# Attention with stationary probabilities, a column of ones beside the values, and two turns before the output projection

## What is computed

```
q, k, v = split(layernorm(x) @ qkv_w.T)          # 12 heads of 16
attn    = softmax(q @ k.T * 16 ** -0.5)
x       = x + (attn @ v) @ proj_w.T + proj_b
```

```
q, k = l2norm(x @ Wq + bq), l2norm(x @ Wk + bk)
attn = softmax(scale * q @ k.T)
out  = (attn @ v) @ Wproj + bproj
```

## Time and profile before

| what | value |
|---|---|
| median of 3 runs | 2835.0 us (2833.94 to 2838.98) |
| the profiled execution | 2838.38 us |
| its span, first to last instruction | 2836.3 us |
| TensorE busy in it | 2164.2 us, 76% |
| VectorE, ScalarE, GpSimd busy | 1301.1, 897.3, 717.6 us |
| mean granted TensorE clock | 0.834 |

### The profile page before, as it was taken

The page is one execution under the profiler, slowest core; times in us unless marked ns, Lnnn a source line. Parts: engine busy times, 40 slices in busy tenths (PEclk is TensorE's granted clock), DMA queues, the critical chain, the costliest instruction groups (busy, mean ns, idle before and its releaser), DMA issues. The chain is left out here.

```text
span 2836.3 us, 45725 instructions
## 1 busy us (share of the span) xinstructions
PE 2164.2 (76%) x13406; PEld 1541.7 (54%) x13406; DVE 1301.1 (46%) x2981; ACT 897.3 (32%) x1857; POOL 717.6 (25%) x728
## 2 busy tenths in 40 slices
PE   9737768775875885886699575777649963999998
PEld 9312225563653774665266531222449952999897
DVE  4359982324454112444311478999542236222222
ACT  1248852222223332232222264555212221121211
POOL 0005530001001452000000016767113430333443
PEclk9658987685885996686799787999769975999999
DMA  7000000000002672000111000000057723677774
GB/s 209 10 0 1 0 0 0 0 0 7 0 0 73 180 198 58 0 0 0 33 47 54 1 0 1 0 0 0 0 161 214 230 63 100 208 216 226 221 211 123
DMA packets 77887, 201.78 MB, mean 71 GB/s; under 512 B 17717, under 2 KB 47288, under 8 KB 69464
## 3 DMA queue, kind: packets, MB, share of 16 engines
q1 hardware_dynamic: 52760, 169.74, 18.4%
q0 software_dynamic: 25056, 31.22, 6.9%
HBM read 179.25 MB, written 22.91 MB: 71 GB/s over the span
## 5 line engine op out<-in xcount | busy, mean ns | idle before, releaser
L1686 POOL DMA_INDIRECT sums<-yblock,put x129 | 206.0, 1597 | 424.3 <-DVE yblock L1949 297.1
L1734 PE MATMUL banks<-xTblock,wt 128*128 128x256 f32 (+1 forms) x1464 | 268.9, 341 | 1.7 <-ACT xTblock L1805 1.2
L1939 DVE TENSOR_TENSOR hid<-sa,banks 128x512 f32<-128x512 f32 (+1 forms) x183 | 105.2, 579 | 352.6 <-ACT sa L1826 206.8
L1759 PE MATMUL banks<-wt,hid 128*128 128x192 f32 x1548 | 266.8, 327 | 0.0
L1759 PEld LDWEIGHTS banks<-wt,hid 128*128 128x128 f32 x1548 | 249.2, 190 | 2.0 <-DVE hid L1939 0.2
L1734 PEld LDWEIGHTS banks<-xTblock,wt 128*128 128x128 f32 x1464 | 236.3, 194 | 24.6 <-issue 1.8
L1826 ACT ACTIVATE sa<-banks 128x512 f32<-128x512 f32 (+1 forms) x183 | 93.0, 510 | 488.0 <-PE banks L1745 382.2
L632 PE MATMUL banks<-g,consts 128*128 128x400 f32 x384 | 184.8, 572 | 60.8 <-DVE g L771 56.8
L740 POOL TENSOR_TENSOR w<-u,spreadB 128x400 f32<-128x400 f32 x192 | 192.7, 1036 | 87.8 <-ACT spreadB L711 87.8
L371 PE MATMUL banks<-consts,xs 100*96 100x100 f32 (+1 forms) x320 | 73.0, 384 | 171.8 <-DVE xs L322 134.1
L1681 POOL DMA_INDIRECT xblock<-table,take x135 | 134.9, 999 | 225.2 <-DVE put L1915 175.3
(11 more groups left out here) (397 smaller groups left out, 3893.3 us busy)
## 6 DMA issues: line engine op xcount, KB each, us to landing
wt<-L3f_packed SPq DMA_DIRECT2D x41, 1152.0 KB
wt<-L3f_packed SPq DMA_DIRECT2D x41, 576.0 KB
wt<-L3m_packed SPq DMA_DIRECT2D x20, 1152.0 KB, 5.5
wt<-L_packed SPq DMA_DIRECT2D x20, 579.0 KB, 5.3
wt<-L3m_packed SPq DMA_DIRECT2D x20, 577.0 KB
wt<-L_packed SPq DMA_DIRECT2D x20, 576.0 KB
pixels<-pixels SPq DMA_DIRECT2D x16, 375.0 KB, 4.6
wu<-L_up SPq DMA_DIRECT2D x8, 576.0 KB, 4.7
```

The lines of the kernel that those rows point to most:

```text
L1686: nc.gpsimd.indirect_dma_start(t.sums, bass.IndirectOffsetOnAxis(put[:, q:q + 1], 0), y[:, b % 2, q - column_of_block[b], :], None, comput ...
L1734: nc.tensor.matmul(bank[:, n * j:n * (j + 1)], wt[:, v, cols(base, 2 * p + j)], xT[:, v, 0, 0:n], start=(j == 0), stop=False, skip_group_c ...
L1759: last = nc.tensor.matmul(bankY[s], hid[:, m, 128 * s:128 * (s + 1)], wt[:, v, DOWN_AT + DIM * m:DOWN_AT + DIM * (m + 1)], start=(m == 0 a ...
L1939: nc.vector.tensor_tensor(hid[:, 2 * p:2 * p + 2, 0:n], sa[:, (PAIRS * v + p) % 2, 0:2 * n].rearrange("p (m n) -> p m n", m=2), second[:, ...
```

## The change

`weigh` exchanges the operands. The exponentials of a head become the stationary operand (100x100), and what moves are 17 columns, the 16 values of the head and a column of ones; there are 12 such products, and they use no strips. The results are queries by features, with the sum of each head in its 17th column. VectorE takes the reciprocal of the 12 sums of a row and multiplies. TensorE turns the result in two halves of 96 features, ScalarE copies them into aT, whose 97th row is of ones for the bias, and the output projection is two products in place of four. In ScalarE's order the copy of aT stands where the logarithm and the exponential stood. The weights of the output projection are laid out in two halves, with the bias in a 97th row.

```diff
--- before.py
+++ after.py
@@ -1293,19 +1293,18 @@
         sq = t.sbuf("sq", [TILE, 2 * HEADS * HEAD], st)
         norm = t.sbuf("norm", [TILE, 3, 2 * HEADS], st)
         v_ = t.sbuf("v", [TILE, 2, HEADS, 2 * HEAD], st)
-        ones = t.sbuf("ones", [TILE, TILE], st)
         qkT = t.sbuf("qkT", [128, 2, GROUPS, TILE], st)
         shiftedT = t.sbuf("shiftedT", [128, GROUPS, TILE], st)
         pT = t.sbuf("probsT", [TILE, 4, GROUPS, TILE], st)
-        logs, inv = (t.sbuf(n, [128, GROUPS, TILE], st) for n in ("logs", "inv"))
-        aT = t.sbuf("aT", [128, GROUPS, TILE], st)
-        wproj = t.sbuf("wproj", [128, GROUPS + 1, DIM], st)
...
+        inv, a = t.sbuf("inv", [TILE, HEADS], st), t.sbuf("a", [TILE, DIM], st)
+        aT = t.sbuf("aT", [HALF + 1, 2, TILE], st)
+        wproj = t.sbuf("wproj", [HALF + 1, 2, DIM], st)
         bankQ, bankV, bankO, bankR, bankS = t.bank[0], t.bank[1], t.bank[2], t.bank[3], t.bank[4:8]
         wholeS = t.psum[0:TILE, 4 * 512:8 * 512].rearrange("p (j n) -> p j n", j=4)[:, :, 0:GROUPS * TILE]
         kT_at = slice(DIM, DIM + GROUPS * TILE)
@@ -1319,8 +1318,7 @@
             @block.gpsimd
             def _(pool):
                 nc.gpsimd.memset(wide[:], 0.0)
-                nc.gpsimd.memset(v_[:], 0.0)
-                nc.gpsimd.memset(ones[:], 1.0).then_inc(cleared, 1)
+                nc.gpsimd.memset(v_[:], 1.0).then_inc(cleared, 1)
 
                 def stage(n, v):
                     nc.gpsimd.tensor_copy(x[:, v], t.xT[0:HALF + 1, :, bass.ds(TILE * n, TILE)]).then_inc(staged, 1)
@@ -1373,13 +1371,11 @@
                     last.then_inc(scoredT, 1)
 
                 def weigh(v):
-                    for bank in (bankR, bankO):
-                        for g in range(GROUPS):
-                            for j in range(4):
-                                rows = slice(32 * j, 32 * (j + 1))
-                                last = nc.tensor.matmul(bank[rows, TILE * g:TILE * (g + 1)],
-                                                        ones[:, 0:2 * HEAD] if bank is bankR else v_[:, v, 4 * g + j, :], pT[:, j, g, :],
-                                                        start=True, stop=True, tile_position=(0, 32 * j))
+                    for g in range(GROUPS):
+                        for j in range(4):
+                            head = 4 * g + j
+                            last = nc.tensor.matmul(bankO[0:TILE, (HEAD + 1) * head:(HEAD + 1) * (head + 1)], pT[:, j, g, :],
+                                                    v_[:, v, head, 0:HEAD + 1], start=True, stop=True)
                     last.then_inc(weighed, 1)
 
                 pe.wait_ge(cleared, 1)
@@ -1393,8 +1389,9 @@
                 pe.wait_ge(staged, 2)
                 project(1)
                 pe.wait_ge(max_done, 1)
-                turn_(0, 0, bankR, 0, shift_turned)
+                turn_(0, 0, bankR, 2 * TILE, shift_turned)
                 pe.wait_ge(wproj_in, 16)
+                pe.wait_ge(ones_done, 1)
                 with pe.Fori(0, TILES // 2) as i:
                     for u in range(2):
                         n = 2 * i + u
@@ -1410,13 +1407,16 @@
                         weigh(u)
                         pe.wait_ge(staged, n + 3)
                         project(u)
+                        pe.wait_ge(a_done, n + 1)
+                        for k in range(2):
+                            last = nc.tensor.transpose(bankR[0:HALF, TILE * k:TILE * (k + 1)], a[:, HALF * k:HALF * (k + 1)],
+                                                       ident[0:TILE, 0:TILE])
+                        last.then_inc(a_turned, 1)
                         pe.wait_ge(max_done, n + 2)
-                        pe.wait_ge(inv_done, n + 1)
-                        turn_(1 - u, 0, bankR, 0, shift_turned)
-                        pe.wait_ge(a_done, n + 1)
-                        for g in range(GROUPS):
-                            nc.tensor.matmul(bankO[0:TILE, 0:DIM], aT[:, g, :], wproj[:, g, :], start=(g == 0), stop=False)
-                        nc.tensor.matmul(bankO[0:TILE, 0:DIM], ones[0:1, :], wproj[0:1, GROUPS, :],
+                        pe.wait_ge(aT_done, n + 1)
+                        turn_(1 - u, 0, bankR, 2 * TILE, shift_turned)
+                        nc.tensor.matmul(bankO[0:TILE, 0:DIM], aT[:, 0, :], wproj[:, 0, :], start=True, stop=False)
+                        nc.tensor.matmul(bankO[0:TILE, 0:DIM], aT[0:HALF, 1, :], wproj[0:HALF, 1, :],
                                          start=False, stop=True).then_inc(out_done, 1)
 
             @block.scalar
@@ -1437,7 +1437,7 @@
 
                 def take_shifted(n):
                     act.wait_ge(shift_turned, n + 1)
-                    nc.scalar.activation(shiftedT[:], bankR[:, 0:GROUPS * TILE].rearrange("p (g n) -> p g n", g=GROUPS),
+                    nc.scalar.activation(shiftedT[:], bankR[:, 2 * TILE:(2 + GROUPS) * TILE].rearrange("p (g n) -> p g n", g=GROUPS),
                                          ACT.Identity).then_inc(shiftedT_done, 1)
 
                 square(0)
@@ -1450,10 +1450,9 @@
                         n = 2 * i + u
                         act.wait_ge(scoredT, n + 1)
                         nc.scalar.activation(pT[:].rearrange("p j g n -> p j (g n)"), wholeS, ACT.Exp).then_inc(exp_done, 1)
-                        act.wait_ge(weighed, n + 1)
-                        nc.scalar.activation(logs[:].rearrange("p g n -> p (g n)"), bankR[:, 0:GROUPS * TILE], ACT.Ln).then_inc(sums_logged, 1)
-                        act.wait_ge(sums_logged, n + 1)
-                        nc.scalar.activation(inv[:], logs[:], ACT.Exp, scale=-1.0).then_inc(inv_done, 1)
+                        act.wait_ge(a_turned, n + 1)
+                        nc.scalar.activation(aT[0:HALF], bankR[0:HALF, 0:2 * TILE].rearrange("p (k n) -> p k n", k=2),
+                                             ACT.Identity).then_inc(aT_done, 1)
                         square(n + 2)
                         take_shifted(n + 1)
                         root(n + 2)
@@ -1472,6 +1471,7 @@
                     else:
                         nc.vector.tensor_copy(place, of.unsqueeze(2).to_broadcast(everywhere))
                 nc.vector.memset(wide[:, :, HEADS:, HEAD + 2], -1.0)
+                nc.vector.memset(aT[HALF:HALF + 1], 1.0).then_inc(ones_done, 1)
 
                 def lengths(n):
                     if unit:
@@ -1522,9 +1522,12 @@
                         n = 2 * i + u
                         take_qkT(n + 1)
                         highest(n + 1, 1 - u)
+                        dve.wait_ge(weighed, n + 1)
+                        weighted = bankO[0:TILE, 0:(HEAD + 1) * HEADS].rearrange("p (h e) -> p h e", e=HEAD + 1)
+                        nc.vector.reciprocal(inv[:], weighted[:, :, HEAD]).then_inc(inv_done, 1)
                         dve.wait_ge(inv_done, n + 1)
-                        nc.vector.tensor_tensor(aT[:].rearrange("p g n -> p (g n)"), bankO[:, 0:GROUPS * TILE],
-                                                inv[:].rearrange("p g n -> p (g n)"), ALU.mult).then_inc(a_done, 1)
+                        nc.vector.tensor_tensor(a[:].rearrange("p (h e) -> p h e", e=HEAD), weighted[:, :, 0:HEAD],
+                                                inv[:].unsqueeze(2).to_broadcast([TILE, HEADS, HEAD]), ALU.mult).then_inc(a_done, 1)
                         lengths(n + 2)
                         take_qk(n + 2, u)
                         take_v(n + 2, u)
@@ -2413,14 +2416,6 @@
     return np.concatenate([a, extra], axis=0)
 
 
-def by_heads(w, bias):
-
-    out = np.zeros((4, 2 * HEAD, HEADS // 4 + 1, DIM), np.float32)
-    out[:, 0:HEAD, 0:HEADS // 4] = w.reshape(HEADS // 4, 4, HEAD, DIM).transpose(1, 2, 0, 3)
-    out[0, 0, HEADS // 4] = bias
-    return out.reshape(128, HEADS // 4 + 1, DIM)
-
-
 def columns(v, parts=HALF):
 
     return np.ascontiguousarray(v.reshape(-1, parts).T)
@@ -2527,13 +2522,13 @@
     for name in ("ln1_g", "ln1_b", "ln2_g", "ln2_b"):
         a["c_L1_" + name] = columns(f["L1_ffn_" + name])
     a["c_L1_qkv"] = halves(f["L1_ffn_qkv_w"].T, np.zeros(3 * DIM, np.float32))
-    a["L1_proj"] = by_heads(f["L1_ffn_proj_w"].T, f["L1_ffn_proj_b"])
+    a["L1_proj"] = halves(f["L1_ffn_proj_w"].T, f["L1_ffn_proj_b"])
     a["c_L1_gate"] = halves(f["L1_ffn_gate_w"].T, f["L1_ffn_gate_b"])
     a["c_L1_b2"] = f["L1_ffn_b2"].reshape(8, 1, DIM)
     a["c_L1_ln2"] = np.concatenate([with_rest(f["L1_ffn_ln2_g"]), with_rest(f["L1_ffn_ln2_b"])], axis=1)
     a["L1_packed"] = stacked([expert_weights([f["L1_ffn_w1"][e].T], f["L1_ffn_w2"][e].T, columns(f["L1_ffn_b1"][e], 128)) for e in range(8)])
     a["c_L2_qkv"] = halves(np.concatenate([f["L2_attn_Wq"], f["L2_attn_Wkv"]], 1), np.concatenate([f["L2_attn_bq"], f["L2_attn_bkv"]]))
-    a["L2_proj"] = by_heads(f["L2_attn_Wproj"], f["L2_attn_bproj"])
+    a["L2_proj"] = halves(f["L2_attn_Wproj"], f["L2_attn_bproj"])
```

(12 more changed lines are left out.)

## The result

The changed kernel takes 2991.9 us (median of 4 runs, 2987.56 to 2996.57) against 2835.2 us: a ratio of 1.0547, interval 1.0529 to 1.0565, or +157 us. Forecast were 2980 and +145. The profiled execution took 2987.6 us; the kernel before took 2838.4 in its own.

What follows compares the result with a forecast made beforehand. TensorE, partly at half clock, was taken to bound both loops. Layer 1's +75, layer 2's +67 and the first tiles' +3 us summed to +145, giving 2980 us (own range 2930 to 3015; with rival 1, 2880 to 3015).

Steps and rivals of the forecast that it cites:

- The clock decides: Both loops: layer 2 at half clock throughout, layer 1 with a sixth of its work at full; +75 and +67 us.
- two causes: TensorE's clock: a longer thin stretch before each fall (2.2 us more), and shorter, interrupted wide work before each rise.
- Rivals 1 and 3: Clock keeps its old share, 2882 us, chance 0.15; weight loads keep both loops at full clock, 2821 us, chance 0.04.
- rival 4: Weight loads hidden and clock as before, gains and waits cancelling: 2835 us, chance 0.03.
- The weighing products: TensorE's weighing stage, 24 instructions at the router's price: +1.05 us a tile at full clock, +1.89 at half.
- The second rival: Weight loads don't slow with the clock, so 24 instructions cost 2.22 us at either: 2937 us, chance 0.11.
- The turns and the wait: TensorE after the projection: two added turns, then a wait for ScalarE's aT copy; +0.76 us at full clock, +0.95 at half.
- The output products: Output projection on TensorE, eight instructions down to four: -0.65 us a tile at full clock, -1.28 at half.
- Layer 2's chain: After the projection, ScalarE's square queues behind the aT copy: +0.70 us at full clock, tile 8.49 to 10.24 us.
- The costs at nothing: VectorE's reciprocal and multiplication lie under the projection; memsets and the wproj transfer in the prologues cost nothing.
- The first tiles' +3 us: First tile of each layer, already at half clock: 2x1.6 us more, counted as +3 us.

Runs made afterwards that it cites:

- filled kernels: Wide idle work in the waits of the kernel before, 2792.9 us; in the changed kernel also 100 columns in its weighing products, 2837.2 us.
- before_add_thin: The kernel before plus 12 idle products a tile ahead of its weighing, loading 100x100 probabilities and moving 17 columns: 2994.8 us, ratio 1.0543.
- after_turn_inside: The changed kernel with the two turns of a between the two halves of the projection: 2964.4 us, ratio 1.0450.
- after_fill_waits: The changed kernel with idle products in its waits alone, weighing products still moving 17 columns: 2931.4 us, ratio 1.0333.
- after_fill_both: The changed kernel with 100 columns moved in the weighing products and idle products in the two waits: 2837.2 us, ratio 0.9995.

## Why the prediction was right

**The clock decides** held, and it is the main step: I had layer 2 at half clock throughout and a sixth of layer 1's work at full. Measured at full were a tenth of layer 2's time and a sixth of layer 1's, which is over a fifth of layer 1's work, as work goes faster there. The filled kernels show the reason, and before_add_thin the direction. Of the prediction's two causes the longer thin stretch is shown; that the shorter output products and the new wait hold the clock down too is not (before_add_thin reaches 0.69 without them, the changed kernel 0.58 with them, and after_turn_inside, without the wait, gains only 0.02 and 0.03 over it). Rivals 1 and 3 (the clock keeps its old share, the loads keep it up) fell with the windows of the changed kernel, and rival 4 (hidden loads) with its weighing products, which take 4.02 us.

**The weighing products** were priced from the router's rows at 2.22 and 4.05 us; they take 2.14 (after_fill_waits) and 4.02. The second rival, loads that don't slow down with the clock, falls: 24 instructions at 168 ns. By the Trainium skill's formula ("TensorE: Matmul & The Clock Gate", section on LDWEIGHTS) a load of 100 columns is an estimated 83 ns; that is near the 89 ns measured at full clock and out by a factor of two at half.

**The turns and the wait** were +0.76 and +0.95 us; they are 0.85 and 1.05. The forecast's 0.06 us for TensorE's resumption was an estimate; behind aT it took 0.14 (800.32 to 800.46), which is most of the difference.

**The output products** were mis-sized, at half clock. I had -0.65 and -1.28 us, half of eight instructions. Two instructions of the old form, those of the product of the ones row, use one row of the array, and the scores of the next tile run among them. What they cost is therefore seen in the next tile, in the time from its scores to the turns of queries and keys. In the kernel before at full clock:

```profile
791.50 0.43 PE L1371 MATMUL banks<-shiftedT,qkT 19*100 19x100 f32 x6
...
792.51 0.73 PE L1349 MATMUL banks<-consts,wide 100*128 100x100 f32 x6
```

That is 1.01 us, and 0.71 in after_fill_both (764.11 to 764.82), 0.30 less. With the 0.33 of the output products themselves (1.08 less 0.75) the full-clock saving is 0.63, near the 0.65 of the forecast. Layer 1's whole full-clock tile grew by 1.20 us (8.05 to 9.25, idle work on both sides), forecast +1.19. But the half-clock tile that I measured, 687.24 to 700.66, was the first one: no such products stood at its start, so nothing of theirs was in the 13.42, and I took them off all the same. Against that tile the saving is only 0.66 us (2.07 in the earlier trace rows, 698.59 to 700.66, less 1.42, 800.99 to 802.41), not 1.28.

These make the half-clock tile: 13.42+1.86+1.05-0.66 and 0.01 of small differences is 15.68, measured 15.69, forecast 14.98. That the total came so close is in part luck. The tile was too short and the share of full clock in layer 1 too small, and the two errors work against each other: with a half-clock tile of 15.69 in both layers and the forecast's shares the same sum gives about +164 us (an estimate from these rows), against the forecast's +145 and the measured +157.

**Layer 2's chain** at full clock was to grow by 0.70 for aT; it grew by 0.39, from 3.04 to 3.43. The turns of a overlap the end of the projection, and ScalarE starts its square 0.23 us after aT's start. Its full-clock period of 10.21, with 0.1 us of idle work in it, matches the forecast's 10.24 by luck: the 8.49 that I started from was the tile right after a half-clock stretch, and the steady tile takes 8.77. The one error, 0.28 too little, hid the other, 0.31 too much. Neither bears much on the total, as layer 2 ran at half clock for nine tenths of the time.

**The costs at nothing** (reciprocal, multiplication, memsets, wproj) were nothing. The first tiles' +3 us came out as +2.6: from the first projection to the first addition it is 29.7 us in place of 27.9 in layer 1 (671.8 to 701.5, 673.5 to 701.4) and 32.1 in place of 31.3 in layer 2 (1195.8 to 1227.9, 1120.4 to 1151.7).

The best version that ran is not the changed one: the kernel before with idle products in its waits, 2792.9 us, or 2796.7 with fewer of them. The changed form with both fills and the turns inside the projection, 2827.5 us, beats the kernel before by 0.5%, and stays 35 us behind the old form filled.

## What to carry to other kernels

When an edit makes products that load much and move little, price the clock beside the products: read what the engine did ahead of each fall and rise, and ask what the edit puts there. Where TensorE sets the pace and runs at half clock in parts, wide products without a use, in waits that it has anyway, are worth a trial. And measure a reference tile at the same place of the cycle as the tile it is compared with, since instructions that run among those of the next tile are paid for there, and a tile behind a change of the clock isn't a steady one.

## What was unexpected

More columns through the same weights made two kernels faster by 98 and 114 us. In the kernel before, 10 to 16 idle instructions a tile gave 1.7%, and 6 to 8 gave 1.6%: its half-clock parts had been a cost that could be removed. And shortening a half-clock tile by 0.5 us left layer 1 as it was, with a clock of 0.55 in place of 0.58.
